# Ten instead of twelve experts ahead of the first scan, and two experts in each of pairs 0 and 2

## The reference

```python
# layer 0: linear attention with decay (16 heads), then a small FFN, then a mixture of 8 experts
x = x + ga * L0_attn(layernorm(x) * (1 + ca) + sa)
logits = xf @ w_router;  probs = softmax(logits);  topk_w, topk_idx = top_k(probs, 2)
weights = sum(topk_w * one_hot(topk_idx))
h   = gelu(einsum('te,ieh->tih', xf, w1) + b1)      # every expert for every token, hidden 512
out = sum((einsum('tih,ihe->tie', h, w2) + b2) * weights)
x = x + gb * out
# layer 1: a state-space scan (256 channels, 16 states), then a Fourier feed-forward
x_val, z = split(x @ W_in.T);  x_val = silu(conv1d(x_val));  dt = softplus(x[:, :, :64] @ W_dt.T + b_dt)
h_t = exp(dt_t * A) * h_(t-1) + dt_t * x_t * B_t;   y_t = sum_n(h_t * C_t)
x = x + ga * ((y * silu(z)) @ W_out.T)
x = x + gb * (real(ifft(fft(x) @ w)) + bias)
```

## Time and profile before

| | us |
|---|---|
| median of 3 runs | 599.6 |
| lowest and highest | 598.94 and 604.6 |
| the profiled execution | 605.89 |
| its span, first to last instruction | 603.9 |
| PE busy in the span | 484.5 |
| DVE busy | 429.1 |
| POOL busy | 348.0 |
| ACT busy | 341.8 |

### The profile page before, as it was taken

The page is one execution under the profiler, slowest core; times in us unless marked ns, Lnnn a source line. Parts: engine busy times, 40 slices in busy tenths (PEclk is TensorE's granted clock), DMA queues, the critical chain, the costliest instruction groups (busy, mean ns, idle before and its releaser), DMA issues.

```text
span 603.9 us, 6833 instructions
## 1 busy us (share of the span) xinstructions
PE 484.5 (80%) x2346; PEld 337.3 (56%) x2346; DVE 429.1 (71%) x723; ACT 341.8 (57%) x455; POOL 348.0 (58%) x248
## 2 busy tenths in 40 slices
PE   3869867679989999989879979889888397677672
PEld 3457545344578887667666767656757243233231
DVE  4766897964534324059898799997998966987951
ACT  0531443224454655589998999979999255343100
POOL 3214977766432132315597667988487955567443
PEclk9986999979999999999999999999999588888796
DMA  8700000000000000301857655658627511211000
GB/s 292 274 1 0 1 1 1 2 0 0 1 0 2 1 2 0 142 1 46 198 115 151 158 137 141 145 117 207 144 74 171 122 54 53 71 69 35 17 0 18
DMA packets 15010, 44.75 MB, mean 74 GB/s; under 512 B 2240, under 2 KB 7744, under 8 KB 12544
## 3 DMA queue, kind: packets, MB, share of 16 engines
q0 software_dynamic: 2448, 17.83, 14.6%
q1 hardware_dynamic: 11952, 25.57, 12.5%
q10 hardware_dynamic: 576, 0.92, 0.5%
HBM read 25.31 MB, written 1.18 MB: 44 GB/s over the span
## 4 chain that ended last, share of the span: by engine, by line
PE 39%; DVE 28%; ACT 11%; POOL 10%; issue 7%; DMA 4%; ACTq 0%; POOLq 0%; DVEq 0%
PE pO L1219 8%; PE pY L1309 6%; DVE Hs L763 6%; DVE S L658 5%; DVE pCT L750 4%; PE pY L1266 3%; POOL ZS L383 3%; DMA Acc<-ZS 3%; PE pH L1207 3%; DVE pH L657 3%; ACT gel L961 3%; ACT dA L973 2%; PE pH L1209 2%; PE pH L1208 2%; POOL ln_x L353 2%
## 5 line engine op out<-in xcount | busy, mean ns | idle before, releaser
L1219 PEld LDWEIGHTS pO<-w_e,gel 128*128 128x128 f32 x1024 | 122.1, 192 | 13.9 <-issue 8.7
L1219 PE MATMUL pO<-w_e,gel 128*128 128x128 f32 x1024 | 124.7, 276 | 1.2 <-DVE X L734 1.0
L763 DVE TENSOR_TENSOR_SCAN Hs<-dA,HL,pCT 128x512 f32<-128x512 f32 x96 | 117.7, 1267 | 7.4 <-POOL Zev L383 3.7
L961 ACT ACTIVATE gel<-pH,b_e 128x512 f32<-128x512 f32 x128 | 86.1, 687 | 40.0 <-PE pH L1209 39.2
L383 POOL TENSOR_TENSOR ZS<-Hs,Crow 128x1024 f32<-128x1024 f32 x32 | 76.7, 2398 | 42.5 <-DVE Hs L763 42.5
L973 ACT ACTIVATE dA<-dt,a_neg 128x512 f32<-128x512 f32 x128 | 81.8, 710 | 15.8 <-DVE Hs L763 15.6
L750 DVE TENSOR_TENSOR pCT<-u,pB 128x1024 f32<-128x1024 f32 x64 | 78.3, 1224 | 16.8 <-PE pB L1291 15.8
L1207 PE MATMUL pH<-h2h,w_e1h 128*128 128x512 f32 x128 | 57.6, 450 | 21.1 <-ACT gel L961 20.1
L383 POOL TENSOR_TENSOR Zev<-Hs,Crow 128x1024 f32<-128x1024 f32 x26 | 62.5, 2408 | 17.3 <-DVE Hs L763 11.7
L734 DVE SCALAR_TENSOR_TENSOR X<-pO,wts,X 128x128 f32<-128x128 f32 x128 | 35.9, 342 | 42.1 <-PE pO L1219 42.0
L439 POOL TENSOR_TENSOR ZA<-Qsb,S 128x1024 f32<-128x1024 f32 x16 | 38.0, 2373 | 35.0 <-DVE S L658 32.7
(11 more groups left out here) (223 smaller groups left out, 882.8 us busy)
## 6 DMA issues: line engine op xcount, KB each, us to landing
Crow<-c_rows SPq DMA_DIRECT2D x32, 512.0 KB, 4.1
Acc<-ZS POOLq DMA_DIRECT2D x10, 1024.0 KB, 8.8
Acc<-Zev POOLq DMA_DIRECT2D x7, 1024.0 KB, 8.4
w_e<-in_w_e SPq DMA_DIRECT2D x2, 2048.0 KB, 10.6
X<-in_x SPq DMA_DIRECT2D x4, 256.0 KB, 7.4
out<-h2T SPq DMA_DIRECT2D x4, 256.0 KB, 2.5
S<-in_w_mod ACTq DMA_DIRECT2D x2, 384.0 KB, 4.9
w_cx<-in_conv_row SPq DMA_DIRECT2D x1, 512.0 KB, 9.5
```

The costliest lines, as they stand in the source:

```text
L763: vec.tensor_tensor_scan(Hs[:, 2 * o + d, 0:w], dA[:, 4 * (p % 2) + 2 * o + d, 0:w], pU[:, d, 0:w], HL[:, d, n:n + 1] if c else 0.0, ALU.m ...
L961: nc.scalar.activation(gel[:, n % NG, 0:w], pH[n % 2][:, 0:w], ACT.Gelu_apprx_tanh, bias=b_e1[:, NK * e + k:NK * e + k + 1]).then_inc(s["m ...
L1219: ins = mm(pO[:, j * P:(j + 1) * P], gel[:, n % NG, j * P:(j + 1) * P], w_e2[:, NK * (g % E) + k, :], start=(k == 0 and j == 0), stop=(k = ...
```

## The change

A table EXPERTS takes the place of p + AHEAD: it gives each pair its list of experts. COUNTS makes the list empty in pairs -4 and -2 and two long in pairs 0 and 2; all other pairs keep one. Experts 8 and 9 are now in pairs -3 and -1, 10 and 11 in pair 0, 12 in pair 1, 13 and 14 in pair 2, and from expert 15 in pair 3 on every expert is where it was. ALONE stays 20. The stages stay in their pairs.

```diff
+COUNTS = {-4: 0, -2: 0, 0: 2, 2: 2}
...
-ALONE = (NL * E - AHEAD) // 2 * 2
+EXPERTS = {p: [] for p in range(-AHEAD - 1, NL * NP + 1)}
+for p in range(-AHEAD, NL * NP):
+    g0 = sum(len(e) for e in EXPERTS.values())
+    EXPERTS[p] = list(range(g0, min(g0 + COUNTS.get(p, 1), NL * E)))
+ALONE = max(p for p in EXPERTS if EXPERTS[p]) + 1
...
             for p, stages in later_stages():
-                g = p + AHEAD
                 scan = 0 <= p < NL * NP
                 if scan:
                     products(2 * p)
                     scans(2 * p)
-                if 0 < g <= NL * E:
-                    moe_acc(g - 1)
+                for g in EXPERTS.get(p - 1, [])[-1:]:
+                    moe_acc(g)
                 run(p, stages, False)
                 if scan:
                     products(2 * p + 1)
                     scans(2 * p + 1)
+                for g in EXPERTS[p][:-1]:
+                    moe_acc(g)
                 run(p, stages, True)
...
                 run(p, stages, "AB")
+                for g in EXPERTS[p][1:]:
+                    hidden(g, range(NK))
                 run(p, stages, "C")
...
                 if moe:
                     down(g, 2)
                     down(g, 3)
+                for h in EXPERTS[p][1:]:
+                    for k in range(NK):
+                        up(h, k)
+                    for k in range(NK):
+                        down(h, k)
                 run(p, stages, "C")
```

More of the change, by code:

```diff
@@ L989, in _ @@
             for p, stages in later_stages():
-                if 0 <= p + AHEAD < NL * E:
-                    hidden(p + AHEAD, (0, 1))
+                for g in EXPERTS[p][:1]:
+                    hidden(g, (0, 1))
                 run(p, stages, "U")
-                if 0 <= p + AHEAD < NL * E:
-                    hidden(p + AHEAD, (2, 3))
+                for g in EXPERTS[p][:1]:
+                    hidden(g, (2, 3))
                 if 0 <= p + 1 < NL * NP:
@@ L1223, in pair @@
             def pair(p, stages):
-                g = p + AHEAD
-                moe = 0 <= g < NL * E
+                moe = bool(EXPERTS[p])
+                g = EXPERTS[p][0] if moe else None
                 if moe:
```

## The result

The changed kernel takes 613.7 us (median of 4 runs, 610.86 to 615.39) against 601.12 us for the kernel before (median of 4, 598.94 to 604.6) in the same comparison. The ratio is 1.02 with a 95% interval of 1.0152 to 1.0247: the change costs about 12 us, 9 to 15 by the interval. In a second group of runs the ratio was 1.0197 (1.0161 to 1.0232, 6 runs against 17), or +11.9 us on 601.82. Slower, as forecast; the forecast difference was +10.2 us, the forecast time 609.8.

The account below looks back on a forecast made before the run. PE was taken to fill pairs -4 to -2, with PE, DVE and ACT nearly full in pairs 0 to 3. 0.0 - 5.7 + 13.4 + 2.5 = +10.2 us on 599.6 gives 609.8; range 604.5 to 614.

Parts of the forecast that it names:

- Pair -4 gives nothing: Lead-in pair -4 without its expert: the layer norm chain behind moe_acc(7) ends at 237.34 as before; 0.0 us.
- Pair -2 gives 5.7: Lead-in pair -2 without its expert: x_part(0, 1) starts earlier and the second softplus comes 5.73 us sooner; 5.7 us gained.
- The doubled pairs cost 13.4: Pairs 0 and 2: each second expert adds a bare expert's 6.73 us behind the old round; 13.4 us lost in all.
- The clock costs 2.5: PE's new 4.1 us pause ahead of ln_turn lowers its clock to 0.50 for some 5.4 us of work; 2.5 us lost.
- second clock rival: The clock falls again in pair -1, behind a 2.4 us pause before up(9, 2); up to 2.5 us more, 612.3; chance 0.13.
- Better hiding: Second experts fill DVE's and ACT's idle time and gelu waits; doubles cost about 8.5 us, whole 604.9; chance 0.05.
- gift of pair -4: The layer norm chain comes forward by the pair's 8.0 us, with no pause or clock fall; 599.3; chance 0.05.

Follow-up runs that it names:

- PE kept busy: Changed kernel plus matmuls of no use in PE's three new pauses (pairs -4, -3, -1), into a bank nothing reads; 611.5 us, 1.0168 against the kernel before.

## Why the prediction was right

- **Pair -4 gives nothing.** Shown three ways: the chain from `moe_acc(7)` to the transposes is 7.28 us in both profiles, PE waits for its end in the changed kernel, and with the clock held L is -5.75 with both pairs emptied and -5.74 with pair -2 alone.
- **Pair -2 gives 5.7.** 5.74 and 5.75 in the two kernels in which the clock held.
- **The doubled pairs cost 13.4.** 6.70 and 6.68 for one, 13.41 for two where the clock held. The changed kernel itself shows 14.0; the 0.6 on top went with the fall at 295.9, and is gone where PE was kept busy. That the second experts add no bound of DVE, ACT or POOL was right as well: where the clock held, the `up(g, 2)` follow the old rounds and the bare expert to within 0.02 us.
- **The clock costs 2.5.** The mechanism holds, since with PE kept busy the clock and 2.6 us came back, but the picture was wrong and that the size came out is in part luck. I expected one pause of 4.1 us and one fall behind it, of some 5.4 us. That is what the kernel with only pair -4 emptied did (4.01 us of pause, 5.3 us of low clock, 2.5 us). In the changed kernel the clock fell already behind `turn`'s pause of 2.12 us, which the prediction had passed over. The trace of before had a hint of this: behind a pause of 1.82 us at 33.11 the clock was at 0.51 from 33.1 to 36.6. With the clock low, `up(8, 0)` and `up(8, 1)` took 2.9 us instead of the 1.6 that two such quarters take at full clock, and closed part of the pause ahead of the transposes to 2.58 us. It fell again there, again in pair -1, as the second clock rival had it (behind a pause of 2.08 us where that rival had 2.4), and in pair 2. The four cost 0, 1.6, 0.4 and 0.6 us, so the 2.5 that the rival put on a second fall was too high. Where the same lead-in ran with three experts in pair 0 and with the gelus ahead of the exps, L was 0.8 us longer than in the two profiles of the changed kernel.
- **The rivals.** Better hiding and the gift of pair -4 did not occur. The softplus starts 257.35 - 257.33 = 0.02 us behind its table load, and the load 256.05 - 256.03 = 0.02 us behind the copy. The drain which the Trainium skill adds to a switch ("ScalarE: Activation LUTs", "What ACT_TABLE_LOAD costs") does not show in the changed kernel either.
- **The level.** 613.7 against 609.8. The kernel before itself came out at 601.1 to 602.1 in later groups and not 599.6, 1.5 to 2.5 us of the gap. What is left, the difference of about 12 instead of 10.2, is inside the interval of the measurement, and isn't explained. It isn't in L + P of the changed kernel, which is +10.2 twice; other executions may pay more for the clock there, as the 0.8 us above show. The parts of the profiles which the change doesn't touch vary by more: `up(1, 2)` starts anywhere from 170.5 to 176.4 us in these ten profiles, with 14 us of low clock ahead of it in the earliest case and 41 in the latest, and the rest behind pair 4 took 294 to 298 us. The two shortest of these, both of the changed kernel (293.8 and 294.3 us), had 41 us of low clock in that part, the two longest, before and only pair -2 emptied (297.9 and 297.8), 55 and 52. That they go together doesn't show which brings about the other.

## What to carry to other kernels

Before moving work out of a full stretch of one engine, look for chains on other engines that end exactly when that engine arrives: a wait of zero in the profile can be a wait that is just covered, and then the work is worth nothing there, while the same work two pairs further on can be worth most of its time (here 5.7 of 6.7 us). Work added to a stretch in which two engines already take turns cost its whole length here, in both orders that were tried. Where totals scatter by a per cent, distances between two fixed instructions in the profile settle tenths of a microsecond that the totals don't, as long as the granted clock is read beside them.

## What was not expected of the hardware

Short pauses were enough for the clock. In the changed kernel PE stood 2.12, 2.58 and 2.08 us, and the clock was at 0.50 from 1.4, 1.0 and 1.1 us behind the pause's end; the fourth fall came 0.8 us behind a pause of 1.87. But a pause of 2.15 us in the kernel before was harmless, and in the kernel with only pair -2 emptied, the pauses in pair -1 (2.06 us) and pair 2 (1.87 us) were harmless too. The matmuls around the pause don't tell either. In the kernel with only pair -4 emptied, PE's stream is the changed kernel's to the end of pair -3, `turn`'s pause is as long, and the expert behind it runs at full speed (0.48 us for its first matmul, 0.78 in the changed kernel at 234.81):

```profile
232.69 0.33 PE L1198 MATMUL pY<-ident,wts 128*128 128x128 f32 x1 [2.11 <-DVE wts L726]
...
234.28 0.48 PE L1215 MATMUL pH<-h2h,w_e1h 128*128 128x512 f32 x1
```

So the same pause was followed by a fall in three profiles (the changed kernel twice, three experts in pair 0) and by none in two (this one and the gelus ahead of the exps). What decides it, no run here shows; a forecast of falls behind pauses of some 2 us is a chance and not a sum. The falls lasted 3.4 us each in the changed kernel; those of the earlier trace rows lasted 6.8, of which PE worked for 4.1 to 6.0.

The low clock can also hide itself: the first fall stretched the matmuls ahead of a wait for POOL and cost 0.0 us, the second, behind that wait, 1.6.
